# Cross-attention block: the first two key products of an item issued by terms, and a new order of all engines

## The reference

```
Qh, Kh, Vh = layernorm(x) @ WQ[h],  ctx @ WK[h],  ctx @ WV[h]     # 16 heads
attn = softmax(Qh Kh^T / 8 + mask * -1e9)                        # 100 x 361 per head
x = x + concat_h(attn Vh) @ WO
x = x + qlinear(gelu(qlinear(layernorm(x), W1, b1)), W2, b2)      # 8-bit quantised FFN
```

## Time and profile before

| | us |
|---|---|
| median of 3 runs (lowest, highest) | 1082.04 (1081.27, 1082.40) |
| the profiled execution, device time | 1081.73 |
| its span, first to last instruction | 1079.9 |
| busy PE / PEld / DVE / ACT / POOL | 1019.1 / 650.5 / 937.4 / 862.5 / 766.1 |

### The profile page before, as it was taken

The page is one execution under the profiler, slowest core; times in us unless marked ns, Lnnn a source line. Parts: engine busy times, 40 slices in busy tenths (PEclk is TensorE's granted clock), DMA queues, the critical chain, the costliest instruction groups (busy, mean ns, idle before and its releaser), DMA issues.

```text
span 1079.9 us, 37623 instructions
## 1 busy us (share of the span) xinstructions
PE 1019.1 (94%) x10639; PEld 650.5 (60%) x10639; DVE 937.4 (87%) x2668; ACT 862.5 (80%) x1809; POOL 766.1 (71%) x1106
## 2 busy tenths in 40 slices
PE   3999999999999999999999999999999999997738
PEld 1555566666666666666666666666666666665327
DVE  5776888888898888888888888888888888886997
ACT  3664888888888888888888888888888888886906
POOL 3336778877777887777887778777777777774700
PEclk9999999999999999999999999999999999999969
DMA  8500676666767676666667767666766666673003
GB/s 238 142 1 14 122 141 139 138 138 138 138 138 140 140 140 139 138 138 138 138 139 140 140 136 138 140 138 139 138 138 139 133 137 140 138 144 127 1 0 123
DMA packets 435437, 136.77 MB, mean 127 GB/s; under 512 B 407666, under 2 KB 434390, under 8 KB 435414
## 3 DMA queue, kind: packets, MB, share of 16 engines
q1 hardware_dynamic: 435414, 136.47, 61.1%
HBM read 28.60 MB, written 6.55 MB: 33 GB/s over the span
## 4 chain that ended last, share of the span: by engine, by line
PE 88%; DVE 7%; ACT 2%; issue 1%; DMA 1%; POOL 0%; ACTq 0%; DVEq 0%; SPq 0%; POOLq 0%
PE front L368 21%; PE front L369 19%; PE front L370 19%; PE back L1309 13%; PE front L1287 7%; PE tp L1287 5%; DVE hrange L1138 3%; DVE hrange L1139 3%; DMA xs<-x 1%; PE front L1424 1%; ACT xn L691 1%; PE tp L1424 1%; PE back L1424 0%; PE front L1192 0%; PE front L1213 0%
## 5 line engine op out<-in xcount | busy, mean ns | idle before, releaser
L616 POOL TENSOR_TENSOR hl<-prob,hl 100x361 f16<-100x361 f32 x511 | 428.6, 853 | 74.6 <-ACT hl L748 73.8
L742 ACT ACTIVATE prob<-prob,nmax 100x361 f32<-100x361 f32 x512 | 295.4, 589 | 5.0 <-DVE nmax L985 3.7
L1309 PEld LDWEIGHTS back<-v,pT 128*128 128x128 f16 (+1 forms) x4608 | 167.8, 98 | 32.3 <-issue 9.6
L748 ACT ACTIVATE hl<-prob 100x361 f16<-100x361 f32 x352 | 175.2, 498 | 3.4
L1309 PE MATMUL back<-v,pT 128*128 128x65 f16 (+1 forms) x4608 | 176.9, 193 | 0.8 <-DMA pT<-hl 0.8
L752 ACT ACTIVATE k_h<-front 128x362 f16<-128x362 f32 x256 | 120.5, 471 | 61.8 <-PE front L370 54.2
L368 PE MATMUL front<-ctx_h,wk_h 128*128 128x362 f16 x512 | 164.0, 320 | 2.4 <-DVE v L1045 1.0
L370 PE MATMUL front<-ctx_h,wk_l 128*128 128x362 f16 x512 | 161.7, 316 | 0.0
L369 PE MATMUL front<-ctx_l,wk_h 128*128 128x362 f16 x512 | 161.4, 315 | 0.0
L1045 DVE SCALAR_TENSOR_TENSOR v<-front,v 128x512 f16<-128x512 f32 (+1 forms) x192 | 132.6, 691 | 30.6 <-ACT v L756 29.9
L756 ACT ACTIVATE v<-front 128x512 f16<-128x512 f32 (+1 forms) x192 | 114.4, 596 | 55.4 <-PE front L370 49.8
(11 more groups left out here) (206 smaller groups left out, 2047.4 us busy)
## 6 DMA issues: line engine op xcount, KB each, us to landing
ctx_raw<-ctxT SPq DMA_DIRECT2D x33, 361.0 KB, 3.2
pT<-hl SPq DMA_TRANSPOSE x253, 3.6
xs<-x SPq DMA_DIRECT2D x8, 400.0 KB
q_all<-x SPq DMA_DIRECT2D x32, 100.0 KB
out<-q_all SPq DMA_DIRECT2D x32, 100.0 KB
xb<-out SPq DMA_DIRECT2D x5, 640.0 KB, 8.2
out<-xb SPq DMA_DIRECT2D x25, 128.0 KB, 1.8
q_all<-wq SPq DMA_DIRECT2D x1, 1024.0 KB, 6.8
```

The lines of the kernel that those rows point to most:

```text
L616: pool.tensor_tensor(hl[0:T, n % RT, 1, 0:S], prob[0:T, n % RP, 0:S], hl[0:T, n % RT, 0, 0:S], ALU.subtract).then_inc(s_lo, 1)
L742: act.activation(prob[0:T, n % RP, 0:S], prob[0:T, n % RP, 0:S], ACT.Exp, bias=nmax[0:T, n:n + 1], scale=-1.0).then_inc(s_exp, 1)
L748: act.activation(hl[0:T, h % RT, 0, 0:S], prob[0:T, h % RP, 0:S], ACT.Copy).then_inc(s_ha, 1)
L1309: ins = pe.matmul(obank[j % 2][:, n % GH * DV:(n % GH + 1) * DV], pT[0:r, n % RT, part_ * ST + st, :], v2[half][0:r, st, v, n % HT, :], st ...
```

## The change

Two things. First, K0 and K1 of an item, which are always neighbours in the new order, are issued together: before the first matmul PE waits for both banks; then come, for K0 and K1, the four terms each that need only `ctx_h` (waiting for ACT's count `s_ch`), then for K0 and K1 the two terms each that need `ctx_l` (waiting for POOL's count `s_c`). The number of matmuls stays.

```diff
-                if kind == "K":
+                if kind == "K" and n == 0:
+                    assert jobs[g + 1] == ("K", 1, later)
+                    if g >= 1 or part != "first":
+                        had = (before + jobs)[g + 1]
+                        bank_read(had[0], had[1], b + had[2])
+                    two = [(banks[("K", m)], slice(m * P, (m + 1) * P)) for m in range(2)]
+                    for m, (dst, ms) in enumerate(two):
+                        for k in range(KD):
+                            if m == 0:
+                                wait(pe, s_ch, KD * a + k + 1)
+                            pe.matmul(dst[:, 0:SE], wk_h[:, k, ms], ctx_h[:, k, :], start=k == 0, stop=False)
+                            pe.matmul(dst[:, 0:SE], wk_l[:, k, ms], ctx_h[:, k, :], start=False, stop=False)
+                    for m, (dst, ms) in enumerate(two):
+                        for k in range(KD):
+                            if m == 0:
+                                wait(pe, s_c, KD * a + k + 1)
+                            ins = pe.matmul(dst[:, 0:SE], wk_h[:, k, ms], ctx_l[:, k, :], start=False, stop=k == KD - 1)
+                        ins.then_inc(s_kp, 1)
+                elif kind == "K" and n > 1:
                     ms = slice(n * P, (n + 1) * P)
                     for k in range(KD):
-                        if n == 0:
-                            wait(pe, s_c, KD * a + k + 1)
                         ins = split3(pe, ps[:, 0:SE], (wk_h[:, k, ms], wk_l[:, k, ms]),
```

Second, all five tables are replaced. Of DVE's, for example:

```diff
-    K=(-5.893, -5.648, -4.835, -3.797, -0.261, 0.688, 2.418, 4.814),
-    V=(-2.725, -2.274, -0.679, 1.492, 6.435, 6.987),
...
-    MAX=(-3.586, -3.558, -3.405, -3.008, -1.096, -0.776, 0.566, 0.613, 2.019, 3.178, 4.599, 6.349, 7.567, 8.998,
-        10.111, 10.476),
...
+    K=(-5.214, -5.149, -2.764, -2.285, 2.39, 3.252, 5.602, 7.687),
+    V=(-1.437, -0.589, 2.156, 4.44, 7.911, 8.612),
...
+    MAX=(-2.455, -2.265, -1.478, -1.174, -0.421, 1.643, 3.088, 3.23, 4.356, 4.593, 5.506, 6.361, 8.249, 8.299,
+        9.554, 10.086),
```

More of the change, by code:

```diff
@@ L87 @@
 PE_STEPS = at(
[L88 to L94, removed]
-ACT_STEPS = at(
[L96 to L105, removed]
@@ L106 @@
-DVE_STEPS = at(
-    K=(-5.893, -5.648, -4.835, -3.797, -0.261, 0.688, 2.418, 4.814),
-    V=(-2.725, -2.274, -0.679, 1.492, 6.435, 6.987),
-    WO=(19.53, 20.987),
-    MAX=(-3.586, -3.558, -3.405, -3.008, -1.096, -0.776, 0.566, 0.613, 2.019, 3.178, 4.599, 6.349, 7.567, 8.998,
-        10.111, 10.476),
[L112 to L117, removed]
@@ L118 @@
-SP_STEPS = at(
[L119 to L123, removed]
-POOL_STEPS = at(
[L125 to L132, removed]
+    K=(-5.991, -5.99, -5.224, -4.29, -0.964, 2.53, 4.215, 5.107),
@@ new lines @@
+    V=(-2.926, -2.252, -1.7, 2.762, 6.339, 6.556),
+    QP=(-4.444, -4.443, -1.855, -1.854, 3.274, 3.275, 7.201, 7.202),
+    PV=(3.638, 3.707, 5.01, 5.857, 8.298, 9.191, 9.814, 10.037, 10.27, 10.449, 13.552, 14.144, 15.309, 15.888,
+        16.79, 16.962),
+    WO=(20.081, 20.604),
+    CT=(-17.857,))
+ACT_STEPS = at(
+    K=(-3.842, -2.405, -1.606, -0.81, 3.313, 6.106, 7.62, 8.029),
+    V=(0.187, 1.227, 2.51, 7.147, 8.802, 9.103),
+    EXP=(-0.259, 1.083, 1.553, 1.605, 2.995, 5.041, 6.605, 7.105, 7.405, 7.831, 7.975, 8.313, 11.001, 11.608,
+        13.758, 15.112),
+    HA=(0.949, 1.397, 1.811, 3.713, 6.909, 7.245, 7.935, 8.75, 11.734, 12.88, 15.411),
+    AH=(11.324, 14.877, 20.796, 21.707),
+    YN=(24.853,),
+    MG=(-1.306,),
+    C=(-5.759, -5.702),
+    Q=(-4.813, -3.605))
@@ new lines @@
+DVE_STEPS = at(
+    K=(-5.214, -5.149, -2.764, -2.285, 2.39, 3.252, 5.602, 7.687),
+    V=(-1.437, -0.589, 2.156, 4.44, 7.911, 8.612),
+    WO=(21.089, 22.412),
+    MAX=(-2.455, -2.265, -1.478, -1.174, -0.421, 1.643, 3.088, 3.23, 4.356, 4.593, 5.506, 6.361, 8.249, 8.299,
+        9.554, 10.086),
+    HV=(0.511, 3.468, 5.131, 7.726, 13.107),
+    NORM=(7.753, 10.816, 17.253, 18.916),
+    CMAX=(-18.416,),
+    CRED=(-16.422,),
+    SCALE=(-12.299,),
+    LN=(22.547, 23.04, 25.111, 25.585))
+SP_STEPS = at(
+    DT=(3.276, 3.332, 6.641, 7.324, 11.705, 13.008, 13.57, 14.183),
+    AD=(15.94, 21.295),
+    CTX=(-18.757,),
+    OUT=(25.229,),
+    X=(13.955,))
@@ L133 @@
+POOL_STEPS = at(
+    LO=(-0.024, 0.336, 2.491, 2.716, 2.865, 7.831, 8.492, 9.065, 9.686, 9.767, 10.763, 12.04, 14.443, 14.512,
+        15.193, 15.213),
+    AL=(14.277, 15.584, 20.36, 22.589),
+    C=(-3.3, -2.79),
+    Q=(-2.44, 0.811),
+    RSTD=(25.807,),
+    CS=(-6.897,),
+    M=(23.177,))
 JOBS = {step: t for step, t in PE_STEPS.items() if step[0] in ("K", "V", "WO")}
@@ L149 @@
 EARLY, LATER = slice(0, 3), slice(3, None)
-LAST_PE = [("PV", n) for n in range(6, 10)] + [
+LAST_PE = [("PV", n) for n in range(7, 10)] + [
     ("PT", 10), ("KW", 0), ("PT", 11), ("KW", 1), ("PT", 12), ("KW", 2), ("PT", 13), ("PT", 14), ("PV", 10), ("PV", 11),
@@ L155 @@
 LAST_ACT = [
-    ("HA", 7), ("EXP", 12), ("AH", 0), ("EXP", 13), ("HA", 8), ("EXP", 14), ("HA", 9), ("EXP", 15),
+    ("EXP", 12), ("AH", 0), ("EXP", 13), ("HA", 8), ("EXP", 14), ("HA", 9), ("EXP", 15),
     ("HA", 10), ("PC", 11), ("PC", 13), ("AH", 1), ("AC", 0), ("AH", 2), ("AC", 1), ("AH", 3), ("YM", 0), ("YN", 0)]
 LAST_DVE = [
[1 row of a table removed]
[1 row of a table added]
     ("NORM", 2), ("NORM", 3), ("DAL", 3), ("AC", 2), ("AC", 3), ("WO", 0), ("WO", 1), ("LN", 0), ("LN", 1),
     ("LX", 0), ("LX", 1), ("LE", 0), ("LM", 0), ("LM", 1)]
-LAST_SP = [("X", 0), ("OUT", 0)]
+LAST_SP = [("DT", 4), ("X", 0), ("OUT", 0)]
 LAST_POOL = [
```

## The result

The changed kernel takes 1106.16 us (median of 4 runs, 1105.14 to 1106.57) against 1082.22 before: ratio 1.0221, 95% interval 1.0203 to 1.0239, slower. The profiled execution took 1106.57, its span is 1104.7 us, 24.8 more than before. The forecast of 1095 had the sign and the places, but 11 us too little, and the time lies outside its range.

What follows compares the result with a forecast made beforehand. PE's stream was taken to bound each 27.30 us turn, with DVE only 10% spare. Turns of 27.82 gave +15.8 us, the ends +0.4 and -1.9; +14.3 on 1081.73 made 1096, less 1 gave 1095, range 1082 to 1102.

Steps and rivals of the forecast that it cites:

- K0 at X + 2.59: PE between items: K0 starts 2.59 us after X, the end of PE's V5; PE itself would be there at 1.94.
- V5's place, the main term: DVE reads V5 only after MAX12 and MAX13, whose scores PE issues after V5; PE stands 0.65 us before each K0.
- MAX12 0.43 after that: Hand-over from PE to DVE: MAX12 starts 0.43 us after QP6's last pair; bounds 0.2 and 0.6.
- K2 too early: PE reaches K2 before K0's bank is free at 2.90 us after K0: stop 0.22 instead of 0.06, bounds 0 and 0.6.
- The 1 us taken off: Whole kernel: 1 us subtracted because PE's stops give DVE and POOL time in which other small stops vanish.
- Own range: The forecast's own range, 1087 to 1102 us, from MAX hand-over (-7 and +5) and tail (0 to 3).
- Terms first: K0 and K1 on PE: the 0.11 us stop for ctx_l goes, and separating equal weights costs nothing.
- V4, WO1, the transposes: PE's later banks: V4's 0.17 us stop goes; WO1 counted 0 (0.3 if late), earlier transposes 0 (0.2 if late).
- The ends: First turn some +0.4 us at K2; last turn MAX15 about 3.7 us after V5's end, attention ending 1.9 us sooner.
- The sum: Whole kernel: 31 turns +15.8, first turn +0.4, last turn -1.9, together +14.3 us.
- the waits go and V5's does not come: Rival at PE before K0: the old stops go without a new V5 stop, 1070 to 1077 us; chance 0.14.
- DVE falls behind for good: Rival: DVE cannot catch up and WO1, K6, K3 are read late, turn +0.8 to +0.9, 1107 us; chance 0.08.

Runs made afterwards that it cites:

- e1: Changed kernel with one rank altered, so that DVE reads V5 before MAX12 and MAX13: 1088.80 us, ratio 1.0064 to the kernel before.
- e5: Changed kernel with K1's bank waited for before K1's first matmul, V5 read between MAX12 and MAX13, and PV6 behind K1: 1076.43 us.
- e2: Changed kernel with the wait for K1's bank moved from before K0's first matmul to before K1's first: 1085.56 us.
- e3: Changed kernel's new order with K0 and K1 issued the old way, one after the other: 1092.61 us.
- e9: e5 with K0 and K1 issued the old way, one after the other: 1101.43 us.
- e4: Kernel before, in its old order, with the new paired issue of K0 and K1: 1092.33 us.
- e7: Old order with the pair, PV6 and PV7 moved behind K1, and DVE's NORM1 behind MAX14: 1100.59 us.
- e10: e7 with DVE's NORM1 moved behind MAX15 instead of MAX14: 1079.69 us, ratio 0.9983 to the kernel before.
- e8: e5 with DVE reading V5 before MAX12 instead of between MAX12 and MAX13: 1089.18 us.
- e11: Changed kernel with PE's loop cut before PV6 instead of before K0, same cyclic order: 1106.28 us.
- e12: e5 with PE's loop cut before PV5 instead of before K0: 1076.74 us.

## Why the prediction was wrong

The mechanism and its two places were forecast rightly. The steps that failed are two sizes, K0 at X + 2.59 (measured 2.78) and K2 at 2.90 after K0 (measured 3.02), and the range that was put around them.

- *V5's place, the main term:* right in mechanism. Each link is in the trace: DVE idle for PE before MAX12, V5 third, PE idle for DVE's v; e1 and e5 take the wait away, e2 most of it. Its size was off, in two steps above all. "MAX12 0.43 after that" was 0.51 (516.48 to 516.99), for which I had taken the hand-over to ACT as nearest row, and "PE goes on 0.05 later" was 0.14. The pitch of MAX and V5 was 0.52 instead of 0.51. Together K0 stood at X + 2.78 instead of X + 2.59: 0.19 a turn, 5.9 us.
- *K2 too early:* right in mechanism, and also too small. K2 stood 3.02 after K0 instead of 2.90, because ACT took K0's result up 0.53 after its last matmul's start instead of 0.43. 0.12 a turn, 3.7 us. The pair is not the reason: this hand-over is 0.52 (median of the turns) in e3 and e9 too, which have the new order and no pair, and 0.43 in e4, e7 and e10, which have the pair in the old order. What in the new order makes it longer is open.
- *The 1 us taken off* for stops that would vanish elsewhere had no row behind it, and no run shows such a gain. With these three, 1095 becomes 1105.6, against 1106.16.
- *Own range:* it was too narrow by the prediction's own terms. The text kept 0.3 us a turn for WO1 and 0.2 for AD1 "in the range" and gave K2's stop a bound of 0.6 instead of 0.22, but the range of 1087 to 1102 adds up MAX's hand-over and the tail alone. K2's bound by itself is worth 0.38 x 31 = 12 us more. Every other hand-over was held fixed, though the kernel before already shows that they differ: its K7 goes over to an idle ACT in 0.35 (498.99 to 499.34), its K0 in 0.43.
- *Terms first:* right, the wait for ctx_l is gone, and the weight loads cost nothing. The forecast named K1's bank as a new wait of K0, but gave the pair no price of its own: e2 shows that 0.68 of the 0.83 us a turn goes when PE waits for that bank only before K1's first matmul. (e1 gives back 0.57 of the same 0.83 from DVE's side; the two overlap.)
- *V4, WO1, the transposes:* right. V4's stop is gone (513.48 directly behind a PV), WO1 waits 0.04, no PV or WO stood for a DMA in the loop.
- *The ends:* last turn right: V5 ends at 993.95, MAX15 is at 997.68, 3.73 later (predicted 3.7), and from V5's end to the program's end it is 110.75 instead of 112.57 us, 1.8 less (predicted 1.9). First turn: K2 stood 3.09 after K0 instead of 2.47, more than the 0.4 of the forecast, but K0 itself began 0.45 earlier (98.41 against 98.86), and the first CT is only 0.2 later. The first K0 lies between 97.4 and 99.2 in the kernels of this document, so little can be read from it.
- *The sum:* 31 turns of 27.82 against 27.30 are 16.1 us, not 15.8. The 0.6 us for which the prediction has DVE idle before MAX12 stand before V5's reading (504.06 in the earlier trace rows). Neither changes the outcome.
- *Rivals:* "the waits go and V5's does not come" was priced at 1070 to 1077; e5, in which V5 does not come late and K2 is covered, is 1076.43. "DVE falls behind for good" had the time (1107) but not the cause, so its fit is luck: DVE is less busy than before (129.8 us of 150, before 134.6), and it waits for PE.

## What to carry to other kernels

Where several in-order engines pass items round, look for the step that sits in one engine's queue behind work that a later step of the waiting engine must first make possible (here V5 behind MAX12, whose scores PE issues after V5). Its price is the length of that whole chain, steps and hand-overs together (here 2.78 us from V5 to K0), less the work that the waiting engine has for that time (here 1.94 by its own pitches), and such work is free while the chain lasts. Waiting for two buffers before the first use of either moves the later wait forward by the work in between; wait where each is first written, and after every move recount all that stands ahead of the step on each engine, not only the step that was moved.

## What the runs showed of the hardware

- In the changed kernel a hand-over from PE to an idle DVE took 0.51 us from the start of the last pair of matmuls (362 columns) to DVE's start, one to an idle ACT 0.35 to 0.53 from the start of the last matmul (K7: 513.06 to 513.41; V4, 512 columns: 514.56 to 514.98; K0: 520.25 to 520.78), from DVE's end to PE's next load 0.05 (e2) or 0.14 (K0 in the changed kernel).
- The jump of the hardware loop right before K0 cost PE 0.06 to 0.09 us (e2, e5, e8) or 0.15 us (e1, e7, e10) where K0 waited for no engine, and nothing that the trace shows where PE stood for DVE anyway (e11) or where the jump stood before a PV (the kernel before, e4, e12).
- Twelve key matmuls in the order high, high, low took the pitch of before: from 518.86 to 520.72 is 1.86 us, 0.155 each, with a weight load each.
- A pass through QP costs PE 0.09 at its start (515.86 + 0.22 = 516.08 to 516.17) and about as much at its end (the last pair starts at 516.95, + 0.154 = 517.10, to 517.20).
